# First attention with the first half's routing and the shared expert: one hand-kept order of steps per engine, in place of a fixed step pattern with insertions

## The chip, the cores and the metric

One NeuronCore of a Trainium2 chip runs the whole kernel. The metric is the device time of one execution in microseconds (us). A core has five engines with their own instruction streams: TensorE (PE; its weight loads are listed as PEld), VectorE (DVE), ScalarE (ACT), GpSimd (POOL) and SyncE (SP, which issues most DMAs). Each engine takes its instructions in the order in which the program lists them and waits at semaphores for the others.

## The reference, cut to what matters

A two-layer decoder on 16 sequences of 128 tokens with 128 features. The change lies between the second and the third line:

```
x = x + L0_attn(layernorm(x))                        # gated recurrence with its feed-forward
x = x + L0_xattn(layernorm(x), ctx, ctx, mask)       # attention: 16 heads of 8, rotary
x = x + L0_ffn(layernorm(x))                         # shared expert + 8 experts, top 2
x = x + L1_attn(layernorm(x))
x = x + L1_xattn(ctx, ctx, layernorm(x), mask)
x = x + L1_ffn(layernorm(x))
```

with, inside `L0_xattn` and `L0_ffn`,

```
scores = einsum('bhqd,bhkd->bhqk', qh, kh) / sqrt(8)
out = einsum('bhqk,bhkd->bhqd', softmax(masked scores), vh)
concat @ Wo + bo
...
shared = (silu(x @ shared_gate.T) * (x @ shared_up.T)) @ shared_down.T
probs = sigmoid(x @ router_w.T + routing_bias);  scores, indices = top_k(probs, 2)
combined = sum over the two experts of score * ((silu(x @ gate_e) * (x @ up_e)) @ down_e)
```

## The kernel before, in words

**Attention (`attention(0)`, a = 0).** It runs over 8 steps n, each of two sequences with all 16 heads. The queries and keys of a step, split into three bf16 parts, lie in DRAM (`q_scr`, `k_scr`) and are loaded into one of three slots. Each engine has its own list of small pieces of work, named here by kind, number and step, as in A3.2 (kind A, number 3, step 2):

- PE: A0 to A7 are groups of scores of four heads each (`scores`, L2070), each with one matmul of the identity ahead of it (`keep_warm`, L1854); M turns the row maxima (`m_rows`, L2114); B0 to B3 are the transposed scores, which contain the maxima by way of rows written into the query slot (`scores_T`, L2088); V0 to V3 are exponentials times values (`values_sum`, L2104); X0, X1 transpose the products (`products_T`, L1746); o0, o1 transpose the normalised heads (`out_rows`, L2129).
- DVE: x0 to x7 reduce the groups A0 to A7 to maxima (L1363); P splits the maxima in two bf16 parts (L1369, L1370); E copies the turned maxima (L1374), after which SP writes them into the query slot (L462) and issues the loads of the step after the next (L434, L436); N0, N1 normalise (L1384, L1386).
- ACT: e0 to e3 are the exponentials of B0 to B3 (L955); K0, K1 copy the products out (L965); s0, s1 store the output (L970).
- POOL: c0, c1 lay out the values (L637).

A1.n and the later groups take turns in two PSUM banks, B in two pairs of banks, V writes bank U, and M, X and o take turns in the single bank T: a piece that writes T waits until the reader of the piece before it in T is done.

**The order of the pieces.** A table `STEP[0]` gives the order of the pieces within a step, the same for all engines; an engine does those of the pieces that are its own. A piece of step n stands together with some of step n + 1 (the A, P, M and E of n + 1) and n - 1.

**Mixture steps.** Output projection, residual, layer norm, router and shared expert of `L0_xattn` and `L0_ffn` are done in four blocks of four sequences. Their steps are named by kind and block. In the order of their dependence: po (PE, output projection, 2 passes, L1782), oc (ACT, L1016), bk (PE, turned back, L1778), ad (DVE, added to x, L1457), sa and sb (DVE, statistics, L1461 to L1467), rs (POOL, 1/sqrt, L657, L658), nr (DVE, normalise, L1472), tr (PE, transpose, L1778), nt (ACT, L1019), ro (PE, router, L2016), lg (DVE, L1477). From nt the shared expert goes on: sg and su (PE, gate and up, L2036), sl (ACT, silu, L1028), hd (DVE, product, L1547), so (PE, down, L2044), sd (DVE, added to x, L1550). From lg of two blocks the routing of half of the tokens goes on: pr (ACT, L1022), ta and tb (DVE, the best two experts, L1485 to L1496), cu (PE, counts, L2022, L2023), cc (DVE, L1499), ps (DVE, places of the rows, L1502 to L1524), te (DVE, the expert of each tile, L1529 to L1533), wt (DVE, weights, L1535 to L1537). gc (DVE) copies the weights of the first three tiles' experts (`gu_copy`, L1434, L1437).

A mixture step of an early block is put behind a named piece of the attention by the table `BESIDE` ("4A6": "tr.0" puts tr.0 behind the place of A6 in step 4's pattern); what is left stands in the three parts of the list `CLOSE` behind and between the last pieces. `ORDER`, which the waits between mixture steps are counted from, is made of both tables.

**What follows.** POOL scatters the normalised rows of the first eight sequences to their places in DRAM (16 indirect DMAs, L711, after ps.0; rs.3 stands between the first eight and the last eight), SP loads them back (L470), and a loop over 46 tiles of routed rows begins on PE (L2220 gate and up, L2232 down), ACT (L1058) and DVE (L1437 copies an expert's weights, L1571 the product). Tile x needs the product of tile x - 2 (L1571); tiles 0 and 1 need sd.2 and sd.3.

## Time and profile before

| | |
|---|---|
| median of 3 runs | 776.41 us (775.45 to 781.89) |
| the profiled execution | 780.67 us, of which the span of its instructions 778.9 us |
| PE busy over the span | 77% |
| VectorE, ScalarE, GpSimd busy | 56%, 38%, 30% |
| mean granted TensorE clock | 0.878 of full speed |
| first attention, first piece to last value sum | 127.8 to 243.8 us |
| from there to the third routed tile on PE | 243.8 to 291.0 us |

Times are microseconds from the first instruction of the profiled execution. Of TensorE's clock, 1.00 is 2.4 GHz and 0.50 is 1.2 GHz; a value between them is a mix of the two over a stretch. PE's matmuls are pipelined, and the profile models their ends, so a piece's price on PE is read as the distance from its start to the start of the next piece while PE does not wait.

### The profile page before, as it was taken

What the parts mean: (1) busy time and instruction counts of PE and PEld (TensorE: products, weight loads), DVE (VectorE), ACT (ScalarE), POOL (GpSimd) and SP (SyncE); (2) the same over time, 40 slices, a digit from 0 to 9 for tenths busy, and PEclk for the clock granted to TensorE, in tenths of its full rate; (3) what the DMA queues carried; (4) which work ended last, traced back from release to release, by engine and by line L of the source; (5) the groups of instructions that cost most, each with busy time, mean ns of one, the idle gap of its engine ahead of it and who ended that gap; (6) DMA issues with size and microseconds to landing.
All of it is one profiled execution on the core that took longest, in us unless ns stands there. A gap on an engine that the chain in (4) does not pass through costs nothing.

```text
span 778.9 us, 15307 instructions
## 1 busy us (share of the span) xinstructions
PE 601.5 (77%) x4751; PEld 432.5 (56%) x4751; DVE 438.5 (56%) x1165; ACT 296.2 (38%) x679; POOL 232.9 (30%) x324
## 2 busy tenths in 40 slices
PE   4699996898778849898716699846799987555992
PEld 2444453665555639798504488623466764534992
DVE  4889787566554554356334566355455642568443
ACT  2585320455334314343202277511145453101661
POOL 6735333001004545243621111022100001353452
PEclk9899998899996989999866899976799997657997
DMA  9955987543200083432100000108543500003014
GB/s 286 323 93 155 274 216 221 130 115 84 66 4 21 30 313 96 122 107 67 47 24 1 0 2 1 50 14 239 131 114 84 127 2 1 0 32 105 25 35 129
DMA packets 87492, 75.71 MB, mean 97 GB/s; under 512 B 10456, under 2 KB 80752, under 8 KB 84512
## 3 DMA queue, kind: packets, MB, share of 16 engines
q1 hardware_dynamic: 82544, 66.80, 31.7%
q0 software_dynamic: 3296, 6.79, 2.9%
q10 hardware_dynamic: 1584, 1.26, 0.5%
q8 instruction: 37, 0.61, 0.3%
q14 instruction: 31, 0.25, 0.1%
HBM read 41.59 MB, written 32.98 MB: 96 GB/s over the span
## 4 chain that ended last, share of the span: by engine, by line
PE 44%; DVE 20%; issue 11%; DMA 7%; POOL 6%; ACT 3%; SPq 3%; another core or an unknown queue 2%; DVEq 2%; POOLq 0%; ACTq 0%
PE ps L2220 5%; PE ps L2104 4%; PE ps L1782 3%; PE ps L1746 3%; PE ps L2088 2%; PE ps L2070 2%; SPq L426 2%; POOL xs_scr L779 2%; PE ps L2323 2%; PE ps L2232 2%; DMA q_scr<-parts 2%; PE ps L1930 2%; PE ps L2066 2%; PE ps L2083 2%
## 5 line engine op out<-in xcount | busy, mean ns | idle before, releaser
L1363 DVE TENSOR_REDUCE negm<-ps 128x4 f32<-128x512 f32 x128 | 85.1, 689 | 63.0 <-PE ps L2070 60.6
L955 ACT ACTIVATE wa<-ps 128x1024 f32<-128x1024 f32 x64 | 65.6, 1025 | 83.0 <-PE ps L2088 80.8
L2220 PE MATMUL ps<-nT,f 128*128 128x128 f32 x368 | 52.3, 287 | 11.3 <-DVE wb L1571 8.4
L2220 PEld LDWEIGHTS ps<-nT,f 128*128 128x128 f32 x368 | 47.1, 200 | 13.7 <-DVE wb L1571 10.0
L2104 PE MATMUL ps<-wa,f 128*32 128x128 f32 x1024 | 42.9, 294 | 2.9 <-ACT wa L955 1.9
L1854 PE MATMUL ps<-identb 128*128 128x512 bf16 x108 | 38.6, 418 | 4.8 <-issue 2.1
L2070 PE MATMUL ps<-stack 75*128 75x128 bf16 x384 | 40.6, 232 | 0.0
L2070 PEld LDWEIGHTS ps<-stack 75*128 75x128 bf16 x384 | 32.4, 105 | 14.6 <-issue 4.8
L711 POOL DMA_INDIRECT x_scr<-y_tok,selT x32 | 31.5, 985 | 28.0 <-ACT stack L1064 18.8
L2088 PE MATMUL ps<-stack 75*128 75x128 bf16 x384 | 35.5, 231 | 2.2 <-DMA stack<-mT 1.5
L784 POOL DMA_INDIRECT y_scr<-f,stack x23 | 25.8, 1121 | 31.5 <-DVE f L1721 21.1
L1058 ACT ACTIVATE wa<-ps 128x256 f32<-128x256 f32 x46 | 17.8, 388 | 44.8 <-PE ps L2220 42.1
L2088 PEld LDWEIGHTS ps<-stack 75*128 75x128 bf16 x384 | 28.9, 104 | 10.2 <-issue 2.8
L2104 PEld LDWEIGHTS ps<-wa,f 128*32 128x32 f32 x1024 | 26.1, 115 | 12.6 <-issue 5.5
L1100 ACT ACTIVATE wa<-ps,rec 128x128 f32<-128x128 f32 x92 | 26.3, 371 | 17.3 <-PE ps L2323 17.3
L1437 DVE COPY f<-w_gu 128x512 f32 x46 | 20.8, 452 | 20.0 <-issue 14.0
L1746 PE MATMUL ps<-ident,xn_tm 128*128 128x128 f32 x32 | 8.9, 432 | 29.8 <-DVE xn_tm L1129 26.3
L1571 DVE TENSOR_TENSOR wb<-wa,ps 128x256 f32<-128x256 f32 x46 | 19.2, 417 | 22.1 <-ACT wa L1058 19.3
L965 ACT ACTIVATE f<-ps 128x512 f32<-128x512 f32 x32 | 19.1, 598 | 32.0 <-PE ps L2104 31.8
L637 POOL COPY f<-v2x 128x144 f32 x16 | 4.9, 307 | 85.1 <-ACTq L963 84.5
L2232 PE MATMUL ps<-w_down,wb 128*128 x184 | 29.7, 286 | 0.7 <-ACT stack L1064 0.5
L637 POOL COPY f<-v0x 128x144 f32<-128x144 f32 x16 | 4.8, 306 | 82.9 <-ACTq L963 82.6
(391 smaller groups left out, 1508.8 us busy)
## 6 DMA issues: line engine op xcount, KB each, us to landing
k_scr<-parts SPq DMA_DIRECT2D x48, 192.0 KB, 3.0
q_scr<-parts SPq DMA_DIRECT2D x48, 192.0 KB, 3.5
stack<-k_scr SPq DMA_DIRECT2D x12, 600.0 KB, 7.0
stack<-q_scr SPq DMA_DIRECT2D x12, 600.0 KB, 5.3
w_w<-in_w SPq DMA_DIRECT2D x2, 2048.0 KB
x_scr<-sel SPq DMA_DIRECT2D x2, 1472.0 KB, 10.3
x_scr<-stack SPq DMA_DIRECT2D x10, 256.0 KB, 4.9
wb<-q_scr SPq DMA_DIRECT2D x4, 600.0 KB, 5.0
```

Of the source, the lines that this page charges most:

```text
L711: g.indirect_dma_start(x0_scr[h], bass.IndirectOffsetOnAxis(ap=pos0_i[:, k * B + b:k * B + b + 1], axis=0), y_tok[:, b, :], None).then_inc ...
L784: g.indirect_dma_start(y_scr, bass.IndirectOffsetOnAxis(ap=xs[:, x, D:D + 1].bitcast(i32), axis=0), ys[:, x, :], None).then_inc(ys_scatter ...
L955: link.release(act.activation(wa[:, u % 2, :], BF[u % 2], ACT.Exp, scale=SCALE), hWA.filled, hWA.at(stage, n * 4 + u), hB.freed)
L1100: last = act.activation(gelu_of[x % NW1][:, c * S:(c + 1) * S], A[x % 2][:, c * S:(c + 1) * S], ACT.Gelu, bias=b1_of[x % NW1][:, c:c + 1])
L1363: v.tensor_reduce(negm[:, g4 * 4:g4 * 4 + 4, j], A[u % 2].rearrange("p (h k) -> p h k", h=4), AX.X, ALU.max, negate=True).then_inc(hA.free ...
L1746: last = tr(T[:, j * S:(j + 1) * S], src(j), ident[:, :])
L1854: mm(bank, identb[:, :], identb[:, :].unsqueeze(1).broadcast_to([128, 4, S]), start=True, stop=True)
L2070: last = mm(bank[:, q * S:(q + 1) * S], qst[s][0:NROW, h, j * S:(j + 1) * S], kst[s][0:NROW, h, j * S:(j + 1) * S], start=(a == 0), stop=T ...
L2088: last = mm(bank[:, q * S:(q + 1) * S], kst[s][0:NROW, h, j * S:(j + 1) * S], qst[s][0:NROW, h, j * S:(j + 1) * S], start=(a == 0), stop=True,
L2104: last = mm(U[rows, cols], v_batch[j][:, h * VC:h * VC + 32], wa[:, u % 2, q * S:(q + 1) * S], start=True, stop=True)
L2220: last = mm(A[x % 2][:, c * S:(c + 1) * S], gu_of[x % NGU][:, c * S:(c + 1) * S], nT[:, k % 2, q * S:(q + 1) * S], start=True, stop=True)
L2232: last = mm(Bk[y % 2][:, 1, 0:D], hid_of[y % NGU][:, c * S:(c + 1) * S], w["down"][:, 1:, c, :][:, bass.ds(chosen, 1), :].rearrange("p o d ...
```

## The change

Both tables go. In their place stands `WOVEN`, with for each engine one list of all pieces of the first attention and all mixture steps, piece by piece. The lists hold the same pieces as before on each engine (198 on PE, 136 on DVE, 78 on ACT); no instruction of the attention or of a mixture step is added or taken out, and the identity matmul ahead of each group of scores stands in both kernels. The second attention keeps its pattern. Beside the order, four things differ:

- po.2, bk.2, tr.2 and ro.2 use the second score bank (A[1]); before, po.2 and bk.2 used T, tr.2 and ro.2 used U.
- The 16 scatters of the first half are two named steps of POOL's list, fa.0 and fb.0; one short GpSimd instruction that stood ahead of them now stands behind.
- x0 of a step waits also until the last maxima were turned into parts, which is the same engine's own earlier work.
- so.1, which writes A[1], waits also for lg.2, which reads it.

```diff
+        def of_attention(step):
+            return step[1].isdigit()
-        ORDER = {eng: FRONT[eng] + [s for n in range(NSTEP) for op, u in STEP[0] for s in extra(eng, n, op, u)]
-                 + [s for part in CLOSE[eng] for s in part.split()] for eng in FRONT}
+        ORDER = {eng: FRONT[eng] + [s for s in WOVEN[eng] if not of_attention(s) and s[:2] not in ("fa", "fb")]
+                 for eng in FRONT}
...
+        T_TURN = {s: k for k, s in enumerate(s for s in WOVEN["PE"] if s[0] in "MXo" and of_attention(s))}
...
-            return U if step in ("tr.2", "ro.2", "bk.3", "ro.3", "cu.1") else T
+            return dict(T=T, U=U, Z=A[1])[bank_name(step)]
+        def bank_name(step):
+            return "Z" if step in ("po.2", "bk.2", "tr.2", "ro.2") else "U" if step in ("bk.3", "ro.3", "cu.1") else "T"
...
+                    for s in WOVEN["POOL"]:
+                        if of_attention(s):
+                            copies(int(s[3]), int(s[1]))
+                        elif s in ("fa.0", "fb.0"):
+                            first_rows("ab".index(s[1]))
+                        else:
+                            mixture_step(s[:-2], int(s[-1]))
...
+            def first_rows(part):
+                g.wait_ge(zero0_stored, 32)
+                g.wait_ge(dve_front, after("ps.0"))
+                for b in range(part * HB // 2, (part + 1) * HB // 2):
+                    scatter(b, 0)
...
+                    if a == 0 and u == 0 and n > 0:
+                        v.wait_ge(mp_ready, n)
...
+                    if n == 1:
+                        pe.wait_ge(dve_front, after("lg.2"))
...
+                if a == 0:
+                    for s in WOVEN["PE"]:
+                        kind, n = s[:-2], int(s[-1])
+                        if not of_attention(s):
+                            mixture_step(kind, n)
+                            continue
+                        u = int(kind[1])
+                        if kind[0] == "A":
+                            scores(n, u, n % 3, n // 3)
+                        elif kind[0] == "B":
+                            scores_T(n, u, n % 3)
...
-BESIDE = {
-    "PE": {"3A6": "po.0", "3B2": "bk.0", "4A6": "tr.0", "4A7": "ro.0", "4B2": "po.1", "5A0": "bk.1", "5B2": "tr.1",
...
+WOVEN = {
+    "PE": """
+            A0.0 A1.0 A2.0 A3.0 A4.0 A5.0 A6.0 A7.0 A0.1 A1.1 M0.0 A2.1 A3.1 A4.1 A5.1 A6.1 B0.0 A7.1 B1.0
...
```

What this does to the instructions is shown at three places. A line number is one of the file it stands in; the same work has other numbers in the two files (scores L2070 and L2077, transposed scores L2088 and L2095, value sums L2104 and L2111, identity L1854 and L1862).

The first place is PE in the middle, where tr.0, ro.0 and po.1 are done. Before, from A6 of step 5 on (L1778 is tr.0, L2016 ro.0, L1782 po.1):

```order
L1854 MATMUL ps<-identb 128x512
L2070 MATMUL ps<-f,wb 128x128 x4
L1778 MATMUL ps<-ident,y_tok 128x128 x4
L2104 MATMUL ps<-wa,f 32x128 x8
L1854 MATMUL ps<-identb 128x512
L2070 MATMUL ps<-f,wb 128x128 x4
L2016 MATMUL ps<-w_router,nT 128x8 x4
L2088 MATMUL ps<-stack 128x128 x8
L1782 MATMUL ps<-y_tok,w_wo 128x512
L2088 MATMUL ps<-stack 128x128 x8
```

Now, from A6 of step 5 on (L1790 is po.1, L1786 tr.0):

```order
L1862 MATMUL ps<-identb 128x512
L2077 MATMUL ps<-f,wb 128x128 x4
L1790 MATMUL ps<-y_tok,w_wo 128x512
L1862 MATMUL ps<-identb 128x512
L2077 MATMUL ps<-f,wb 128x128 x4
L2095 MATMUL ps<-stack 128x128 x16
L1786 MATMUL ps<-ident,y_tok 128x128 x4
```

po.1 moved ahead of tr.0, and ro.0 moved out of the step, behind five groups of scores of the next.

The second place is PE at the end of the attention. Before, from X0.7 on (L2036 x4 is sg.0 with su.0, the second L1746 X1.7, L1778 tr.2, L1782 po.3, L2016 ro.2, L2044 so.0):

```order
L1746 MATMUL ps<-ident,f 128x128 x4
L2104 MATMUL ps<-wa,f 32x128 x8
L2129 MATMUL ps<-ident,o_tok 128x128
L2104 MATMUL ps<-wa,f 32x128 x8
L2036 MATMUL ps<-nT,w_gu 128x512 x4
L1746 MATMUL ps<-ident,f 128x128 x4
L1778 MATMUL ps<-ident,y_tok 128x128 x4
L2129 MATMUL ps<-ident,o_tok 128x128
L1782 MATMUL ps<-y_tok,w_wo 128x512
L2036 MATMUL ps<-nT,w_gu 128x512 x2
L2016 MATMUL ps<-w_router,f 128x8 x4
L2044 MATMUL ps<-w_down,wb 128x128 x8
```

Now, from sg.0 on (L2027 and L2028 are cu.0, the second L2041 su.0, the second L1754 X1.7):

```order
L2041 MATMUL ps<-nT,w_gu 128x512 x2
L1754 MATMUL ps<-ident,f 128x128 x4
L2111 MATMUL ps<-wa,f 32x128 x16
L2027 MATMUL ps<-pick,earlier 128x64
L2028 MATMUL ps<-pick,ones 128x64
L2041 MATMUL ps<-nT,w_gu 128x512 x2
L2136 MATMUL ps<-ident,o_tok 128x128
L1786 MATMUL ps<-ident,y_tok 128x128 x4
L2041 MATMUL ps<-nT,w_gu 128x512 x2
L1754 MATMUL ps<-ident,f 128x128 x4
L2021 MATMUL ps<-w_router,f 128x8 x4
L2136 MATMUL ps<-ident,o_tok 128x128
```

sg.0 moved ahead of the last value sums, and cu.0, which stood between B2.6 and B3.6, behind them.

The third place is DVE at the end of the mixture steps. Before, from the last copy of gc.0 on (L1550 is sd.2, L1547 hd.3, L1499 cc.1, the second L1550 sd.3, L1502 the start of ps.1):

```order
L1437 COPY f<-w_gu 128x512
L1550 TENSOR_TENSOR x_tok<-x_tok,ps 128x512
L1547 TENSOR_TENSOR wb<-wa,ps 128x1024
L1499 COPY xn_tm<-ps 128x128
L1550 TENSOR_TENSOR x_tok<-x_tok,ps 128x512
L1502 SCALAR_TENSOR_TENSOR xn_tm<-ones,xn_tm 128x64
```

Now, from the end of tb.1 (L1505) on (L1556 is hd.3, L1508 cc.1, L1511 the start of ps.1):

```order
L1505 TENSOR_TENSOR pick<-pick 128x8x8
L1556 TENSOR_TENSOR wb<-wa,ps 128x1024
L1508 COPY xn_tm<-ps 128x128
L1511 SCALAR_TENSOR_TENSOR xn_tm<-ones,xn_tm 128x64
L1512 TENSOR_TENSOR xn_tm<-xn_tm 128x64
```

and, further on, at the end of te.1 (L1542; L1559 is sd.3, what follows wt.0):

```order
L1540 TENSOR_REDUCE selT<-xn_tm 128x23
L1541 TENSOR_SCALAR selT<-selT 128x23
L1542 CAST selT<-selT 128x23
L1559 TENSOR_TENSOR x_tok<-x_tok,ps 128x512
L1544 TENSOR_TENSOR wsum<-top_p 128x16
L1545 RECIPROCAL wsum<-wsum 128x16
```

sd.3 moved from ahead of ps.1 to behind te.1; gc.0 moved up to between hd.0 and lg.2, sd.2 to ahead of ta.1, and ps.0 with te.0 from ahead of sa.2 to behind nr.2.

## Rows read from the trace of the kernel before

**Rows 1.** Busy time by stretch: stretch, its us, each engine, granted clock, DMA share

```profile
147.70:158.30 10.60, 9.70 (x148) 7.07 (x148) 7.15 (x16) 6.16 (x9) 0.61 (x2) 1.00 0.51 120
158.30:168.60 10.30, 9.66 (x147) 7.09 (x148) 6.72 (x14) 5.52 (x9) 0.61 (x2) 1.00 0.51 123
168.60:181.50 12.90, 11.39 (x154) 7.81 (x153) 7.62 (x16) 6.90 (x10) 0.61 (x2) 1.00 0.39 98
181.50:196.00 14.50, 12.70 (x163) 8.81 (x162) 9.49 (x29) 7.03 (x10) 1.84 (x4) 1.00 0.37 88
196.00:212.60 16.60, 12.48 (x156) 8.74 (x155) 10.07 (x29) 6.45 (x9) 1.81 (x4) 0.91 0.32 77
212.60:229.60 17.00, 14.13 (x161) 10.05 (x161) 10.61 (x31) 6.80 (x10) 0.61 (x2) 0.89 0.01 2
229.60:243.80 14.20, 11.35 (x129) 7.95 (x129) 8.37 (x38) 6.13 (x9) 1.84 (x4) 0.64 0.01 2
```

**Rows 2.** Timeline of PE at full clock: start, us, operation, idle before

```profile
161.44 0.38 PE L1854 MATMUL ps<-identb 128*128 128x512 bf16 x1
...
161.88 0.61 PE L2088 MATMUL ps<-wb,f 75*128 75x128 bf16 x8
162.32 0.38 PE L1854 MATMUL ps<-identb 128*128 128x512 bf16 x1
...
163.75 0.64 PE L2104 MATMUL ps<-wa,f 128*32 128x128 f32 x16
164.33 0.33 PE L2129 MATMUL ps<-ident,o_tok 128*128 128x128 f32 x1
...
184.21 0.63 PE L1746 MATMUL ps<-ident,f 128*128 128x128 f32 x4 [0.38 <-ACTq L95]
...
222.98 1.10 PE L1782 MATMUL ps<-y_tok,w_wo 128*128 128x512 f32 x2 [0.28 <-ACTq L95]
```

**Rows 3.** Groups of instructions, 127 to 284 us: count, busy, mean ns, idle before

```profile
L1363 DVE TENSOR_REDUCE negm<-ps 128x4 f32<-128x512 f32 x64 | 42.9, 689 | 27.1 <-PE ps L2070 25.1
L955 ACT ACTIVATE wa<-ps 128x1024 f32<-128x1024 f32 x32 | 32.8, 1025 | 37.9 <-PE ps L2088 35.9 <-ACT wa L955 2.0
```

**Rows 4.** Timeline of VectorE's closing part, idle time before each; then PE's load

```profile
234.27 0.29 DVE L1502 TENSOR_TENSOR_SCAN xn_tm<-ones,xn_tm 128x64 f32<-128x64 f32 x1
...
239.33 0.49 DVE L1461 BATCH_NORM_STATS2 bn<-x_tok 128x6 f32<-128x128 f32 x2 [0.24 <-DVE selT L1533]
...
243.15 1.11 DVE L1472 TENSOR_SCALAR y_tok<-x_tok,mv,rstd 128x128 f32<-128x128 f32 x4 [0.94 <-POOLq L659]
...
249.76 0.26 DVE L1384 RECIPROCAL rec<-ps 128x16 f32<-128x16 f32 x1 [5.50 <-issue]
...
255.03 0.19 DVE L1477 TENSOR_TENSOR rl<-ps,rbias 128x32 f32<-128x32 f32 x1 [3.25 <-PE ps L2036]
...
257.36 0.69 DVE L1457 TENSOR_TENSOR x_tok<-x_tok,ps 128x512 f32<-128x512 f32 x1 [2.13 <-PE ps L1778]
...
281.94 0.69 DVE L1550 TENSOR_TENSOR x_tok<-x_tok,ps 128x512 f32<-128x512 f32 x1 [3.09 <-PE ps L2044]
...
290.53 0.41 DVE L1571 TENSOR_TENSOR wb<-wa,ps 128x256 f32<-128x256 f32 x1
291.00 1.78 PEld L2220 LDWEIGHTS ps<-nT,f 128*128 128x128 f32 x8 [5.61 <-DVE wb L1571]
```

**Rows 5.** Timeline of GpSimd's scatters and SyncE's load; its landing time, median us

```profile
244.57 1.24 POOL L711 DMA_INDIRECT x_scr<-y_tok,selT  x1 [0.98 <-DVEq L1551]
...
262.87 1.03 POOL L711 DMA_INDIRECT x_scr<-y_tok,selT  x1 [0.88 <-POOL rstd L658]
...
274.24 1.43 SPq L470 DMA_DIRECT2D stack<-x_scr  x2
...
stack<-x_scr SPq DMA_DIRECT2D x2, 256.0 KB, 2.8
```

**Rows 6.** The chain that ended last: one load of a step's keys

```profile
149.88 8.29 DMA stack<-k_scr
```

192 lines of the change are left out of this document (102 added, 90 removed), and 16 rows, old and new, of tables (BESIDE, CLOSE, STEP).

## The prediction

> **What bounds the kernel now.** I read the busy time by stretch first, cut at the starts of the steps on PE [rows 1]. In the two steps that hold no mixture step (147.7 to 168.6) a step takes 10.6 and 10.3 us, and PE is busy 9.70 and 9.66 of them: 93%. These steps are bound by PE, with VectorE at 7 us. The steps with mixture steps take 12.9, 14.5, 16.6 and 17.0 us, and the last value sums another 14.2: from 168.6 to 243.8 there are 75.2 us, in which PE is busy 11.39 + 12.70 + 12.48 + 14.13 + 11.35 = 62.05 (83%), VectorE 46.2. No engine is full there: they wait for each other in turn. In the group table VectorE sat idle 27.1 us before them and ScalarE 37.9 us before its exponentials [rows 3]. The granted clock says a second thing: 1.00 up to 196.0, then 0.91, 0.89 and 0.64, so part of the later stretches ran at 1.2 GHz. The timeline of the closing part says a third: VectorE carries the chain to the routed loop, and sits idle in it for 5.50, 3.25, 2.13 and 3.09 us; the loop's third tile starts at 291.00, after a PE wait of 5.61 us for the first product on VectorE (290.53) [rows 4].
>
> So the change acts on three pieces: the steps up to 168.6, the middle (75.2 us) and the closing part (243.8 to 291.0, 47.2 us). Everything behind 291.0 follows in the same order and shifts with it.
>
> **Prices on PE.** From starts at full clock: a group of scores with its identity 161.44 to 161.88, 0.44; a B 161.88 to 162.32, 0.44; a V 163.75 to 164.33, 0.58. An X is four transposes, at most the 0.63 of its row, I take 0.5; po is 1.1 [rows 2]. The o and M are single transposes, 0.15 (estimate, a quarter of X). A plain step is 8 A, 4 B, 4 V, 2 X, 2 o and M: 3.5 + 1.8 + 2.3 + 1.0 + 0.5 = 9.1 us, against the 10.3 measured, a factor of 1.14.
>
> **The change, part by part.**
>
> *The start.* B0.0 waits for SyncE's write of the turned maxima, in both orders. Now three more groups of scores stand ahead of it (A4.1 to A6.1), work that was to be done anyway, while B0.0 itself gets at most one group later. M comes one to three V and X earlier in steps 1 and 2, which starts SyncE's load earlier. Gain: 0 to 3 us. I take 0.5, since PE was already busy 93% in the steps that follow.
>
> *The middle.* No work is added, so I cost what may be recovered. Were all waits as short as in the plain steps, the 62.05 us of busy PE would take 62.05/0.93 = 66.7 us: 8.5 less. The part at 1.2 GHz, twice (1 minus granted): 2 x (0.09 x 16.6 + 0.11 x 17.0 + 0.36 x 14.2) = 17.0 us, in which PE did the work of 8.5. With PE denser this could go too, so the most to be had is 17 us. The least is nothing. To choose between them I count the new lists by stretch:
> - A0.4 to A0.5: 8 A, 5 V, 5 B, po's successor bk.0, 2 X: PE 10.6, VectorE 7.0 (a plain step [rows 1]) plus ad, sa and sb of a block.
> - A0.5 to A0.6: PE 8.7, with two B and two V fewer held back; VectorE 8. The same stretch took 14.5 us before.
> - A0.6 to A0.7: VectorE is the longest. Block work of sa, sb, nr, lg and then ad, sa, sb, nr lies in the two stretches 181.5 to 212.6, whose busy time exceeds two plain steps by 9.49 + 10.07 - 13.9 = 5.7 us, so a block is 3.2 busy, about 4.4 with the pauses between its chained pieces. 7.0 + 0.7 of pauses + 0.7 for a third N + 4.4 = 12.8 us (16.6 before).
> - A0.7 to A7.7: PE 5.6, VectorE 6.6.
> - From there to V3.7: ScalarE is the longest, with eight exponentials of 1.03 [rows 3] and 0.2 of handoff each (estimate from the plain steps), and about 6 us of copies and of pr.0 between them: 16 us.
>
> The longest engine's sum from A0.4 on is 11.2 + 8.7 + 12.8 + 6.6 + 16 = 55.3. Before, measured over the longest engine's count was 12.9/10.4, 14.5/11.6 and 16.6/12.1: 1.24 to 1.37, the last one at a lowered clock. The order was made with handoffs in view (V stands farther behind its B, an X behind other work), and I take 1.15, the factor of the plain steps: 63.6 us instead of 75.2, a gain of 11.6. At 1.25 it is 69.1, a gain of 6; at 1.0, 20.
>
> The bank T is a limit of its own: po, bk, tr and ro hold it from PE's write to the reader's end, about 1.1 + 0.7 + two handoffs of 0.2 for po. The move of po.2 and bk.2 to A[1] takes some 3.7 us of such holds out of it. It costs nothing: A[1] has no group of scores left by then, and A7.7's maximum was read before.
>
> A rule of the Trainium skill is weighed here. "TensorE: Matmul & The Clock Gate", section on HAM oscillation, puts the loss by a lowered clock at the throttled time times one half, 17.0/2 = 8.5 us in this stretch. The rows bear it out only in part: 181.5 to 196.0 ran at 1.00 throughout and still took 1.25 times its longest engine. By the rule alone the middle would gain 8.5; my sum doesn't use it.
>
> *The loads.* SyncE writes M's rows for step n, then issues the loads of step n + 2, whose keys land 8.29 us later [rows 6]; with the issue of both about 10.5 us from E.n to A0.(n + 2). M0.3 is now behind A1.4 and B3.2. From it to A0.5 PE has 6 A, 5 V, 4 B, 2 X, bk.0 and small ones, 9.5 us, so A0.5 may wait 1 us; M0.5 to B0.5 and M0.6 to B0.6 (3.7 and 2.7 us of PE against about 3.7 for turn, copy and SyncE's write) up to 1 us each. Behind a waiting A0.5 stands all of PE. Up to 3 us, inside the factor of 1.15.
>
> *The closing part.* Let V be the end of V3.7 (243.8 before). Before, VectorE went from ps.0 at 234.27 to the end of product 0 at 290.94, 56.7 us [rows 4]. Of it, sa.2, sb.2, N0.7 and nr.2 (239.33 to 244.26, 4.9) now stand ahead of ps.0. N1.7, for which it idled 5.50, now stands behind nr.2, cc.0, ps.0 and te.0, over 6 us of work, so that wait is covered. lg.2 (3.25) has hd.0 and gc.0 ahead of it, ad.3 (2.13) hd.1. sd.3 (3.09), which waited for so.3, stands behind ps.1 and te.1. If that cover failed, each would come back at its own size. All four gone: 14.0. I add 2 for new waits, at hd.2 and hd.3, because sg.3, su.3 and so.2 now come one behind the other on PE. 56.7 - 4.9 - 14.0 + 2 = 39.8. But cu.0 now stands behind V3.7, so ps.0 starts about 2 after V, where before it started 9.5 ahead. The loop's third tile then stands at V + 42, 47.2 before: a gain of 5.4. What follows next is the rows' way: POOL's 16 scatters took 10.1 (244.57 to 254.7) and 9.9, and waited for rs.3 between; without a wait SyncE issues at about ps.0's end + 23.5, and with 2.8 for landing [rows 5] the rows are there at V + 6 + 26.5 = V + 32.5, 9 us ahead of need. Bounds: 0 (all four waits return elsewhere) and 9.
>
> **The sum.** 0.5 + 11.6 + 5.4 = 17.5, rounded to 18. The profiled execution, 780.7, would become 762.7; it lies 4.3 above the median, so 776.4 - 18 = **758.5 us**.
>
> **The rivals.**
> - *The waits only move (B).* An in-order list with waits sized for other durations stalls elsewhere, and the middle gains 0 to 2; the closing waits are separate and go. For it: the steps with mixture work have no full engine, yet were not dense. Against: the stretches after A0.5 lose work outright. 776.4 - 7 = 769.
> - *The closing gain is lost (C).* ps.0 is later against V, and the scatter chain of 26.5 us or rs.3 between gets on the path. It decides once ps.0 ends later than V + 15. Middle alone: 776.4 - 12 = 764.5.
> - *All of it (D).* Factor 1.0 to 1.05 in the middle: -17 to -20, and -8 in the closing: 750.
> - *No effect (E).* Both only shuffle: 776.
> - *Slower, by the clock (F).* From A7.7 on no identity matmuls are left, and more B, V and sg work stands there, 13.6 + about 27 of PE at full clock up to so.3. If the short waits between these keep PE at 1.2 GHz, each us of it costs another. Before, 17.0 of the 48 us ahead of 243.8 were at 1.2 GHz. To end slower the lowered clock must cover over 26 us more than before, for it has to outweigh 18; throughout from A0.6, 55 us of work would take 110, and the kernel about 795. Against it: rows 1 show 1.00 wherever PE was busy over 86%. A rule speaks for it: the same page of the Trainium skill, section "A second HAM failure mode: psum-queue depth-cycling", says that short pauses between groups that cycle PSUM banks make the clock alternate. The plain steps here cycle banks too, and stay at 1.00.
>
> **How the numbers follow.** Forecast (752 to 765): 0.55. B 0.17, C 0.10, D 0.10, E 0.04, F 0.04. Under 1% (7.8 us, about what a measurement of this kernel tells from no change) nothing counts as faster: forecast, C, D and a good third of B are over it, 0.82; the rest of B and E within it, 0.14; F 0.04. For 8 in 10 I leave out E, F, half of D and the slow third of B: 750 to 769.
>
> **What would show it.** In the profile after: steps 2 and 3 at 10 us as before; A0.5 to A0.7 in about 25 us, not 31.1; V3.7's end near 232; granted clock over 0.9 up to there; VectorE's wait before so.3's reader gone and none over 2 us behind ps.0; the third tile near 273. Wrong if the middle keeps 83% of busy PE, if the loads show as PE's releaser for over 3 us, or if ps.0 ends later than V + 8.

## The result and the profile after

The changed kernel takes 759.17 us (median of four runs, 754.92 to 764.65), beside 779.15 us for the kernel before on the same chip (775.45 to 785.72). The ratio is 0.971, with a 95% interval of 0.966 to 0.976: 20 us less, where 18 were forecast (758.5). The profiled execution of the changed kernel took 754.92 us, with a span of 753.2. The ratios in this document leave out executions more than 1.5% above the fastest of the same kernel, which concerns three of the ten of before_no_identity (788.7 to 790.0 us) and no others.

Busy time by stretch, after, cut at the starts of the steps on PE as in [rows 1] (stretch, its us, PE, PE's loads, VectorE, ScalarE, GpSimd, granted clock, DMA share, GB/s). The first row starts with A0.2, the third with A0.4, the last two hold A7.7 to the end of V3.7, and the closing part:

```profile
146.70:157.10 10.40, 9.59 (x147) 6.93 (x147) 6.53 (x15) 5.25 (x7) 0.31 (x1) 1.00 0.38 86
157.10:166.60 9.50, 9.20 (x128) 6.56 (x125) 6.00 (x12) 5.51 (x8) 0.61 (x2) 1.00 0.56 132
166.60:179.95 13.35, 11.66 (x178) 8.56 (x176) 9.62 (x30) 6.87 (x9) 1.84 (x4) 1.00 0.40 97
179.95:189.45 9.50, 9.14 (x120) 6.56 (x117) 7.39 (x17) 5.17 (x8) 0.61 (x2) 1.00 0.53 132
189.45:202.90 13.45, 12.69 (x197) 9.72 (x195) 10.18 (x30) 7.69 (x11) 1.81 (x4) 1.00 0.40 94
202.90:210.30 7.40, 6.12 (x64) 4.25 (x63) 5.08 (x11) 2.00 (x3) 0.31 (x1) 1.00 0.03 6
210.30:228.90 18.60, 14.72 (x219) 10.35 (x217) 9.58 (x37) 11.22 (x17) 1.82 (x4) 1.00 0.01 3
228.90:271.80 42.90, 33.00 (x160) 22.30 (x160) 29.60 (x94) 12.98 (x18) 25.72 (x35) 0.92 0.32 111
```

V3.7 ends at 228.9 (243.8 before), the clock is at its upper level throughout up to there, and the third routed tile starts 42.9 us later (47.1 before). So the kernel is 15 us ahead at the first mark and 19.2 at the second. Everything behind runs the same code; the profiled execution is 25.7 us shorter in the end, but the last 6.5 of it lie behind, in code that didn't change, and the medians differ by 20.0.

The groups of instructions that answer to [rows 3], 127 to 265 us (count, busy, mean ns, idle before): the maxima still number 64, and VectorE sits idle 19.2 us ahead of them instead of 27.1, while ScalarE's idle time ahead of its exponentials is as it was.

```profile
L1372 DVE TENSOR_REDUCE negm<-ps 128x4 f32<-128x512 f32 x64 | 42.0, 687 | 19.2 <-PE ps L2077 16.5 <-DVE bn L1470 0.2
L966 ACT ACTIVATE wa<-ps 128x1024 f32<-128x1024 f32 x32 | 32.7, 1023 | 37.7 <-PE ps L2095 33.5 <-ACT wa L966 1.2 <-PE ps L2111 1.0
```

The timeline of VectorE in the closing part, after (start, us, operation, idle before and its releaser), which answers to [rows 4]:

```profile
228.00 0.26 DVE L1393 RECIPROCAL rec<-ps 128x16 f32<-128x16 f32 x1 [2.93 <-PE ps L1754]
...
230.43 0.29 DVE L1511 TENSOR_TENSOR_SCAN xn_tm<-ones,xn_tm 128x64 f32<-128x64 f32 x1
...
235.57 0.26 DVE L1393 RECIPROCAL rec<-ps 128x16 f32<-128x16 f32 x1 [0.26 <-DVE selT L1542]
...
240.63 0.18 DVE L1486 TENSOR_TENSOR rl<-ps,rbias 128x32 f32<-128x32 f32 x1
...
252.05 0.19 DVE L1486 TENSOR_TENSOR rl<-ps,rbias 128x32 f32<-128x32 f32 x1 [1.21 <-PE ps L2021]
254.44 0.69 DVE L1559 TENSOR_TENSOR x_tok<-x_tok,ps 128x512 f32<-128x512 f32 x1 [2.20 <-PE ps L2051]
...
268.65 0.69 DVE L1559 TENSOR_TENSOR x_tok<-x_tok,ps 128x512 f32<-128x512 f32 x1
```

These are N0.7, ps.0, N1.7, lg.2, lg.3, sd.2 and sd.3. ps.0 stands 1.5 us behind V3.7. N1.7's wait fell from 5.50 to 0.26, and those of lg.2 (3.25) and sd.3 (3.09) are gone; ad.3 has none either. New are 2.20 at sd.2, 1.21 at lg.3 and 2.93 at N0.7.

### The profile page after: what moved, and what is told of

Read it like the earlier page. It is cut to its first block, busy times and chain, and to the rows that moved or that the text cites. A ratio compares the mean times of both kernels' runs of the same rounds, so it can differ in the third digit from the quotient of the medians.

```text
span 753.2 us, 15317 instructions
## 1 busy us (share of the span) xinstructions
PE 588.2 (78%) x4751; PEld 421.9 (56%) x4751; DVE 438.9 (58%) x1165; ACT 294.9 (39%) x679; POOL 232.4 (31%) x324
## 3 DMA queue, kind: packets, MB, share of 16 engines
q0 software_dynamic: 3296, 6.79, 2.9%
## 4 chain that ended last, share of the span: by engine, by line
PE 48%; DVE 19%; issue 11%; DMA 6%; ACT 4%; POOL 4%; SPq 3%; another core or an unknown queue 2%; DVEq 2%; POOLq 0%; ACTq 0%
PE ps L2234 4%; PE ps L2111 4%; PE ps L1790 3%; PE ps L1754 3%; PE ps L2077 3%; PE ps L2095 2%; SPq L432 2%; PE ps L2246 2%; DMA q_scr<-parts 2%; ACT wa L966 2%; PE ps L1938 2%; PE ps L2073 2%; PE ps L2337 2%; PE ps L2090 2%
## 5 line engine op out<-in xcount | busy, mean ns | idle before, releaser
L2234 PE MATMUL ps<-nT,f 128*128 128x128 f32 x368 | 50.6, 281 | 8.9 <-DVE wb L1579 4.8
L2234 PEld LDWEIGHTS ps<-nT,f 128*128 128x128 f32 x368 | 45.6, 195 | 11.2 <-DVE wb L1579 6.1
L1862 PE MATMUL ps<-identb 128*128 128x512 bf16 x108 | 41.0, 436 | 13.3 <-issue 8.1
L2111 PE MATMUL ps<-wa,f 128*32 128x128 f32 x1024 | 39.1, 278 | 4.9 <-ACTq L95 2.2
L2077 PE MATMUL ps<-stack 75*128 75x128 bf16 x384 | 39.1, 226 | 0.0
L2077 PEld LDWEIGHTS ps<-stack 75*128 75x128 bf16 x384 | 31.3, 101 | 13.7 <-issue 3.1
L2095 PE MATMUL ps<-stack 75*128 75x128 bf16 x384 | 33.3, 223 | 0.6 <-DMA stack<-mT 0.6
L1065 ACT ACTIVATE wa<-ps 128x256 f32<-128x256 f32 x46 | 17.7, 385 | 39.8 <-PE ps L2234 39.5
L1107 ACT ACTIVATE wa<-ps,rec 128x128 f32<-128x128 f32 x92 | 26.1, 369 | 16.9 <-PE ps L2337 16.9
L2111 PEld LDWEIGHTS ps<-wa,f 128*32 128x32 f32 x1024 | 24.9, 110 | 12.9 <-ACT wa L966 5.3
L1754 PE MATMUL ps<-ident,xn_tm 128*128 128x128 f32 x32 | 8.8, 431 | 29.9 <-DVE xn_tm L1136 26.3
L2095 PEld LDWEIGHTS ps<-stack 75*128 75x128 bf16 x384 | 26.9, 100 | 8.3 <-issue 2.1
L1579 DVE TENSOR_TENSOR wb<-wa,ps 128x256 f32<-128x256 f32 x46 | 19.2, 418 | 20.3 <-ACT wa L1065 16.1
L1862 PEld LDWEIGHTS ps<-identb 128*128 128x128 bf16 x108 | 11.3, 106 | 30.3 <-issue 21.1
## 6 DMA issues: line engine op xcount, KB each, us to landing
x_scr<-sel SPq DMA_DIRECT2D x2, 1472.0 KB, 10.3
```

The costliest lines, as they stand in the source:

```text
L1107: last = act.activation(gelu_of[x % NW1][:, c * S:(c + 1) * S], A[x % 2][:, c * S:(c + 1) * S], ACT.Gelu, bias=b1_of[x % NW1][:, c:c + 1])
L1754: last = tr(T[:, j * S:(j + 1) * S], src(j), ident[:, :])
L1862: mm(bank, identb[:, :], identb[:, :].unsqueeze(1).broadcast_to([128, 4, S]), start=True, stop=True)
L2077: last = mm(bank[:, q * S:(q + 1) * S], qst[s][0:NROW, h, j * S:(j + 1) * S], kst[s][0:NROW, h, j * S:(j + 1) * S], start=(a == 0), stop=T ...
L2095: last = mm(bank[:, q * S:(q + 1) * S], kst[s][0:NROW, h, j * S:(j + 1) * S], qst[s][0:NROW, h, j * S:(j + 1) * S], start=(a == 0), stop=True,
L2111: last = mm(U[rows, cols], v_batch[j][:, h * VC:h * VC + 32], wa[:, u % 2, q * S:(q + 1) * S], start=True, stop=True)
```

## The experiments

Four marks in the trace of each kernel tell where its time went: E.3, E.6 and E.7 (VectorE's copy of the turned maxima of steps 3, 6 and 7), V (the end of V3.7) and T (the third routed tile on PE). The first column is the time against the kernel before on the same chip. The marks come from one profiled execution each, and V and T are good to about 0.1 us.

| kernel | ratio (95%) | E.3-E.6 | E.6-E.7 | E.7-V | V-T |
|---|---|---|---|---|---|
| before | 1 | 44.0 | 17.2 | 14.0 | 47.1 |
| changed | 0.971 (0.966 to 0.976) | 36.3 | 8.8 | 15.5 | 42.9 |
| tail_old | 0.985 (0.978 to 0.992) | 36.3 | 8.5 | 16.8 | 52.2 |
| mid_old | 0.987 (0.978 to 0.996) | 46.0 | 18.5 | 12.4 | 41.4 |
| splice_e6 | 0.984 (0.979 to 0.990) | 45.1 | 9.7 | 15.4 | 42.5 |
| mix_old | 0.992 (0.990 to 0.995) | 44.5 | 16.5 | 16.6 | 43.4 |
| att_old | 0.995 (0.992 to 0.997) | 44.1 | 18.9 | 16.9 | 42.9 |
| e7_late | 0.979 (0.973 to 0.985) | 36.3 | 12.6 | 18.1 | 41.7 |
| banks_old | 0.978 (0.972 to 0.985) | 36.3 | 8.5 | 19.4 | 42.4 |
| no_identity | 0.973 (0.966 to 0.980) | 35.0 | 11.2 | 16.5 | 42.5 |
| before_no_identity | 0.998 (0.994 to 1.002) | 45.2 | 18.7 | 13.4 | 47.2 |
| before_warm | 0.998 (0.994 to 1.001) | 45.2 | 20.7 | 13.4 | 48.0 |
| sg0_behind_x | 0.970 (0.967 to 0.973) | 36.3 | 8.6 | 15.0 | 41.7 |
| two_moves | 0.973 (0.968 to 0.978) | 36.3 | 8.5 | 16.3 | 42.6 |

E.3 lies between 167.4 and 170.4 in all of them (before 168.70, changed 168.33). One per cent of the ratio is 7.8 us.

### The closing part alone, and the rest alone

tail_old keeps the changed kernel up to N1.7 and puts the order of before behind it. On two of the engines (ScalarE's list is put back in the same way):

```diff
 VectorE, behind N1.7
-hd.0 gc.0 lg.2 hd.1 ad.3 sa.3 sb.3 sd.0 sd.1 nr.3 hd.2 lg.3 sd.2 ta.1 tb.1 hd.3 cc.1 ps.1 te.1 sd.3 wt.0
+hd.0 lg.2 ad.3 sa.3 sb.3 sd.0 hd.1 nr.3 sd.1 hd.2 lg.3 ta.1 tb.1 gc.0 sd.2 hd.3 cc.1 sd.3 ps.1 te.1 wt.0
 PE, behind o0.7
-tr.2 sg.1 X1.7 ro.2 o1.7 po.3 su.1 bk.3 so.0 so.1 sg.2 su.2 tr.3 ro.3 so.2 sg.3 su.3 cu.1 so.3
+X1.7 tr.2 o1.7 po.3 sg.1 ro.2 so.0 bk.3 su.1 sg.2 so.1 tr.3 su.2 ro.3 sg.3 so.2 su.3 cu.1 so.3
```

> The changed kernel with the order of before put back behind o0.7 on PE, N1.7 on VectorE and K1.7 on ScalarE (the closing part alone), the new order up to there. Theory (two separate gains, 15 in the middle and 4.2 in the closing part): the waits of VectorE at lg.2, ad.3 and sd.3 come back (3.25, 2.13 and 3.09 before, less what short new waits of the new tail go), V3.7 still ends near 229, the third tile stands at V + 47, and the kernel takes 4 to 6 us more than the changed one, 764. Rival (the closing gain came only from what was moved ahead of V3.7, not from the order behind it): the third tile at V + 43, within 1.5 us of the changed kernel, 759.

It takes 0.985 of before, some 10 us more than the changed kernel where 4 to 6 were expected, and nearly all of it lies where the order was put back: V stands at 229.6, T 52.2 us behind. VectorE's waits there, in the timeline of tail_old:

```profile
243.28 0.19 DVE L1486 TENSOR_TENSOR rl<-ps,rbias 128x32 f32<-128x32 f32 x1 [4.90 <-PE ps L2041]
246.58 0.69 DVE L1466 TENSOR_TENSOR x_tok<-x_tok,ps 128x512 f32<-128x512 f32 x1 [3.11 <-PE ps L1786]
...
273.07 0.69 DVE L1559 TENSOR_TENSOR x_tok<-x_tok,ps 128x512 f32<-128x512 f32 x1 [3.49 <-PE ps L2051]
```

lg.2, ad.3 and sd.3 wait 4.90, 3.11 and 3.49 us: the same three waits as in [rows 4], each a little larger. The theory had V + 47; it missed that ps.0, which stood 9.5 us ahead of V before, is behind it now (231.21, V + 1.6). From ps.0 to the end of product 0 VectorE takes 50.6 us here; before, it took 56.7, of which 4.9 were pieces that now stand ahead. So the old tail costs 5 us more behind V than it did in its own kernel.

mid_old is the counterpart: the order of before up to V3.7, N1.6 and K1.7, the new one behind.

```diff
 VectorE
-... P0.7 lg.1 E0.7 N0.6 ta.0 tb.0 N1.6 ad.2 sa.2 sb.2 N0.7 nr.2 cc.0 ps.0 te.0 N1.7 hd.0 ...
+... tb.0 x7.7 P0.7 cc.0 N0.6 E0.7 ad.2 N1.6 sa.2 sb.2 N0.7 nr.2 ps.0 te.0 N1.7 hd.0 ...
```

> The counterpart: the order of before up to V3.7 on PE, N1.6 on VectorE and K1.7 on ScalarE, the new order behind it; tr.2 and ro.2 use A[1], po.2 and bk.2 stay on T. Theory: V3.7 ends near 243.8 as before, the closing part gains 3 to 5 us, so 773 to 775 where before is 777 to 779. Rival (closing and middle gains depend on each other, since cu.0, sg.0 and bk.2 have moved between the two): no gain or a loss, 777 or more, with N1.7 or ps.0 waiting for what now stands late on PE.

0.987 of before. V stands at 245.3, 1.5 later than before, and T 41.4 behind it (47.1 before): T is 4.2 us earlier. That is the net gain of the closing part on its own, in the trace, and bears the theory out; the ratio, with its wide interval, would allow 3 to 17. By the ratios the two parts (1.5% and 1.3%) add up to the whole (2.9%); by the traces, 9.1 and 4.2 us at T, 6 of the 19.2 us need both. The intervals don't decide between these.

splice_e6 has the order of before up to M0.6, E0.6, e3.5 and rs.1, and the new one behind.

```diff
 PE
-... X0.5 A0.7 A1.7 M0.6 A2.7 X1.5 A3.7 A4.7 tr.1 A5.7 B0.6 ...
+... tr.1 B3.5 X0.5 V2.5 M0.6 V3.5 A0.7 A1.7 A2.7 X1.5 A3.7 A4.7 A5.7 B0.6 ...
```

> The order of before up to M0.6 on PE, E0.6 on VectorE, e3.5 on ScalarE and rs.1 on POOL, the changed kernel's order behind it. Theory (the gain is made stretch by stretch, and most of it behind E.6): E.6 near 212.7 as before, V3.7 24.3 us after it (31.2 before), third tile 43 after V3.7, so 11 us less than before and 8 to 9 more than the changed kernel, 768. Rival (the new order needs its own state ahead of it, since steps held back before are late behind the cut): E.6 to V3.7 28 us or more, 772 to 777.

768.92 us, 0.984. E.6 stands at 213.2, and V 25.1 us behind it (31.1 before, 24.3 in the changed kernel). So the gain behind E.6 doesn't need the new order ahead of it. Of the middle's gain, 7.7 us are made from E.3 to E.6 and 6.9 behind.

### Is it the clock?

Before, the last three stretches of the middle ran at 0.91, 0.89 and 0.64 [rows 1], and the changed kernel runs them at 1.00. Does the order gain because it keeps the clock up? before_warm tries to buy the clock alone:

```diff
                     pe.wait_ge(hB.freed, hB.at(stage, n * 4 + u))
+                    if a == 0 and n > 4:
+                        keep_warm(Bk[u % 2][:, 0, :], n // 7 + 1)
```

> The kernel before, in its own order, with one more identity matmul of 4 x 128 columns ahead of each of the four B groups of steps 5 and 6, and two ahead of each in step 7: 16 matmuls of 0.22 us, 3.5 us of added PE work; the output is unchanged. Theory (order): the lowered clock from 196 to 243.8 was a consequence of the waits; the waits are between engines and stay, so the added work buys the clock at most in part, and the time is 0 to 3 us longer. Rival (clock): the 17.0 us at 1.2 GHz, in which PE did the work of 8.5, were what the middle lost; with the granted clock at 1.00 the kernel gains 8.5 - 3.5 = 5 us or more though no step is moved.

The time is that of before (0.998, 0.994 to 1.001), and in the profiled execution the clock wasn't bought. Busy time by stretch of before_warm, E.5 to E.6 and E.6 to E.7:

```profile
196.30:213.60 17.30, 14.40 (x160) 9.89 (x159) 10.17 (x29) 6.44 (x9) 1.82 (x4) 0.84 0.29 74
213.60:234.30 20.70, 19.42 (x169) 13.46 (x173) 10.81 (x31) 6.79 (x10) 0.62 (x2) 0.64 0.01 2
```

So this trace says nothing on what a clock at 1.00 would give. It is also the least favourable of the ten executions: its mean clock is 0.868, their median 0.884, and 0.873 is the median of the kernel before's thirteen beside them. In the others some clock may have been bought, then, though no time beyond the interval. mid_old says more on the price of a lower clock, by chance: up to V3.7 it has the order of before, and its clock was lower than before's. The same two stretches of mid_old:

```profile
196.60:214.50 17.90, 14.25 (x156) 10.10 (x155) 10.09 (x30) 6.38 (x9) 1.81 (x4) 0.81 0.29 71
214.50:232.90 18.40, 16.87 (x165) 11.61 (x168) 10.70 (x31) 6.79 (x10) 0.61 (x2) 0.72 0.01 3
```

At 1.2 GHz ran 2 x (0.19 x 17.9 + 0.28 x 18.4) = 17.1 us of them, in the profile of before 2 x (0.09 x 16.6 + 0.11 x 17.2) = 6.8. The two stretches took 36.3 and 33.8 us. So 10.3 us more at the lower clock came with 2.5 us more of time, a quarter, if all of the difference is put down to the clock: PE was busy 31.12 us instead of 26.79, and shorter waits took up much of the difference. A second pair gives less. E.7 to V has the same order in before and in before_no_identity (below), and no group of scores in it: 14.0 us at 0.63 (10.4 us at 1.2 GHz) and 13.4 us at 1.00, so there the lower clock came with 0.6 us. The Trainium skill ("TensorE: Matmul & The Clock Gate", section on HAM oscillation) counts half of the throttled time as lost; that is more than these traces show, where PE is not full. By these two pairs, an estimate, the 17.0 us at 1.2 GHz were worth 2 to 4 of the middle's 15 us.

no_identity takes the identity matmuls away from the changed kernel:

```diff
-                    if a == 0 and True:
+                    if a == 0 and False:
                         keep_warm(bank, 1)
```

> The changed kernel without the identity matmul ahead of each group of scores of the first attention: 64 matmuls of 0.22 us, 14 us of PE work less; the output is unchanged. If the order alone makes the gain, PE is shorter by up to 12 us in the steps bound by it and the kernel is faster, 750 to 759. If the clock is what the identity matmuls buy, the granted clock in the steps falls to 0.5 to 0.8, each us at 1.2 GHz costs up to half, and the kernel takes 10 to 40 us more, 770 to 800.

0.973, where the changed kernel has 0.971: the same within the intervals, and neither of the two expected ranges (750 to 759, 770 to 800) holds its median of 761.0. The granted clock was lower in these two stretches of no_identity (E.6 to E.7, E.7 to V), where the changed kernel has 1.00:

```profile
204.40:215.50 11.10, 10.69 (x99) 9.23 (x100) 5.74 (x14) 3.90 (x5) 0.00 (x0) 0.58 0.02 3
215.50:232.00 16.50, 13.46 (x162) 8.74 (x162) 7.67 (x32) 8.73 (x14) 1.82 (x4) 0.87 0.01 2
```

They hold 2 x (0.42 x 11.1 + 0.13 x 16.5) = 13.6 us at 1.2 GHz, nearly the 17.0 of before, and E.3 to V still takes 62.7 us (75.2 before, 60.6 changed). So 12.5 of the 14.6 us that the order gains there are gained with nearly as much time at 1.2 GHz as before. These 12.5 contain what the missing identity matmuls save; the next kernel takes that out.

before_no_identity is the same edit on the kernel before.

> The kernel before without the identity matmul ahead of each group of scores of the first attention (14 us of PE work less; the output is unchanged). Without it the changed kernel stood at 0.973 of before. If order and identity are independent, this kernel lies within 0.5% of before, 778 to 784, and the order's gain without identity is again 18 us or so. Rival (the old order, with more waits on PE, needs the identity matmuls to keep the clock, and the new one does not): 790 or more.

0.998 (0.994 to 1.002): no measurable difference. E.3 to V takes 77.3 us, against 62.7 in no_identity: without identity matmuls the order gains 14.6 us there, as it does with them. So the gain doesn't hang on them, and at the prices above most of it isn't the clock's either. That leaving them out changes nothing doesn't mean that they do nothing. From E.3 to E.7 before_no_identity has 32 of them fewer and runs 2 x (0.11 x 15.1 + 0.35 x 17.0 + 0.42 x 18.7) = 30.9 us at 1.2 GHz instead of 6.8, and takes 63.8 us instead of 61.2; from E.1 to E.3 it takes 20.0 instead of 20.9. Less work and less clock may cancel.

### The attention's order, or the places of the mixture's steps?

mix_old keeps the attention's pieces in the new order and puts the mixture steps back where they stood. Some of the edits on VectorE:

```diff
 VectorE
-E0.6 x1.7 x2.7 N1.5 x3.7 x4.7 x5.7 x6.7 x7.7 P0.7 lg.1 E0.7 N0.6 ta.0 tb.0 N1.6 ad.2 ... cc.0 ps.0
+E0.6 x1.7 lg.1 x2.7 N1.5 x3.7 x4.7 ta.0 x5.7 x6.7 tb.0 x7.7 P0.7 cc.0 E0.7 N0.6 ad.2 N1.6 ps.0
```

> The changed kernel with the attention's own steps in the new order, but each step of the mixture up to V3.7 put back behind the attention step that it followed before (po.1, tr.1, ro.1, po.2, bk.2, oc.0, oc.2, nt.1 and ad.2 one to four places later, where the bank T's turns leave no other; po.2 and bk.2 on T again). Theory P (places of the mixture's steps make the middle gain, because each of them makes PE wait for a reader when it stands too near its producer): V3.7 ends near 240, and the kernel takes 7 to 11 us more than the changed one, 766 to 770. Rival A (the attention's own order makes it, V farther behind its B): V3.7 within 3 us of 229, 759 to 762.

att_old has the attention as before and the mixture steps behind the neighbours of the changed kernel.

```diff
 PE
-A1.6 V2.4 M0.5 A2.6 V3.4 X0.4 A3.6 A4.6 ro.0 A5.6 B0.5 bk.1 B1.5
+X0.4 V2.4 M0.5 A0.6 V3.4 A1.6 o0.4 A2.6 X1.4 A3.6 B0.5 A4.6 ro.0 bk.1 B1.5
```

> The counterpart: the attention's steps in the order of before, the mixture's steps up to V3.7 behind the attention step that they follow in the changed kernel (ad.0, bk.1, nt.1 and sg.0 moved by one or two places for the turns of the banks); closing part new. Theory P: most of the middle gain is here, V3.7 ends near 232, 760 to 763. Rival A: V3.7 ends at 240 or later, 768 to 772.

Both expectations fell. Neither half makes any of the middle's gain: E.3 to E.6 takes 44.5 and 44.1 us, before 44.0, the changed kernel 36.3; V stands at 245.8 and 250.0. Both kernels also have po.2 and bk.2 back on T and some steps moved by a place or more for the banks' turns, so they aren't pure halves; banks_old below shows no cost of T ahead of E.7. The new tail alone (mid_old) gave at least as much as either. What halves do to each other can be read in mix_old, where ta.0 stands among the maxima, but pr.0, its input, comes from a ScalarE that itself waits for PE. Timeline of VectorE in mix_old:

```profile
217.30 0.69 DVE L1372 TENSOR_REDUCE negm<-ps 128x4 f32<-128x512 f32 x1 [0.16 <-PE ps L2077]
220.52 0.20 DVE L1494 TENSOR_SCALAR pr<-pr 128x64 f32<-128x64 f32 x1 [2.52 <-ACT pr L1029]
...
223.00 1.29 DVE L1372 TENSOR_REDUCE negm<-ps 128x4 f32<-128x512 f32 x2
```

PE's next group of scores waits for these maxima, and ScalarE in its turn waits 6.79 us for PE. The timelines of PE and ScalarE:

```profile
223.75 0.61 PE L1862 MATMUL ps<-identb 128*128 128x512 bf16 x1 [4.17 <-DVE negm L1372]
...
228.19 1.02 ACT L966 ACTIVATE wa<-ps 128x1024 f32<-128x1024 f32 x1 [6.79 <-PE ps L2111]
```

One late input among the maxima held all three engines in turn. That accounts for part of E.6 to E.7 (16.5 us instead of 8.8); which waits make the 8.2 us more from E.3 to E.6 isn't shown here. In the changed kernel ta.0 stands behind E0.7, with nothing of the attention behind it but three normalisations.

e7_late tests that place by itself. Only M0.7 and its reader are moved, behind the neighbours that they had before:

```diff
 PE
-V0.6 V1.6 M0.7 B3.6 o1.5 V2.6 X0.6 po.2
+V0.6 V1.6 B3.6 o1.5 V2.6 X0.6 M0.7 po.2
 VectorE
-P0.7 lg.1 E0.7 N0.6 ta.0
+P0.7 lg.1 N0.6 E0.7 ta.0
```

> The changed kernel with one link of the last score chain put back by a few places: M0.7 on PE behind X0.6 instead of ahead of B3.6, and its reader E0.7 on VectorE behind N0.6 instead of ahead of it, as the two stood to each other before. Theory C (E.n sets the pace: its write to memory releases all of B.n and so ScalarE's exponentials, and the gain of E.6 to E.7, 17.2 to 8.8 us, comes from E0.7 having neither N0.6 nor the mixture's pieces ahead of it): E.7 3 to 4 us later, V3.7 as much, 762 to 763. Rival (the exponentials have slack there): V3.7 within 1 us of E.n as before, 759.

0.979, 6 us more than the changed kernel by the ratios, whose intervals overlap; 5.1 us from E.3 to T in the traces. E.6 is unmoved, E.7 comes 3.8 us later (12.6 instead of 8.8), and V another 2.6 (18.1 instead of 15.5). VectorE's timeline in e7_late: P0.7, lg.1, then N0.6 waits 3.93 us for X0.6, with E0.7 behind it.

```profile
210.78 0.19 DVE L1379 TENSOR_TENSOR mp<-negm,mp 128x32 bf16<-128x32 f32 x1
210.98 0.19 DVE L1486 TENSOR_TENSOR rl<-ps,rbias 128x32 f32<-128x32 f32 x1
215.11 0.26 DVE L1393 RECIPROCAL rec<-ps 128x16 f32<-128x16 f32 x1 [3.93 <-PE ps L1754]
...
216.27 0.22 DVE L1383 COPY mT<-ps 64x128 bf16<-64x128 bf16 x1 [0.41 <-PE ps L2121]
```

In the changed kernel P0.7's last piece stands at 212.03 and E.7 at 213.41, 1.4 us later; here it is 5.5. E.n releases the write to memory, and with it all of B.n and the exponentials, and in this trace what stands between P and E came out at V in full and more. The theory holds, and its size (3 to 4) was short by 2.6 at V: the granted clock in the stretch behind was 0.72 instead of 1.00 as well.

### The bank

banks_old takes po.2 and bk.2 back to T, tr.2 and ro.2 to U. In the changed order bk.2 can't use T as it stands: X1.6 behind it would wait for ad.2, which on VectorE stands behind X1.6's own reader. So X1.6 goes first:

```diff
-return "Z" if step in ("po.2", "bk.2", "tr.2", "ro.2") else "U" if step in ("bk.3", "ro.3", "cu.1") else "T"
+return "U" if step in ("tr.2", "ro.2", "bk.3", "ro.3", "cu.1") else "T"
 PE
-B0.7 B1.7 bk.2 X1.6 V0.7
+B0.7 B1.7 X1.6 bk.2 V0.7
```

> The changed kernel with po.2 and bk.2 back on the bank T and tr.2 and ro.2 on U as before; X1.6 stands ahead of bk.2, since behind it X1.6 would wait for a reader that stands behind X1.6's own. Theory (the move to A[1] costs nothing and takes 3.7 us of holds out of T): 1 to 4 us more than the changed kernel, 760 to 763. Rival (the holds lie beside the exponentials, which set that stretch): within 1 us, 759.

0.978, 5 us more than the changed kernel (the intervals overlap). The trace places it: E.7 to V takes 19.4 us instead of 15.5, everything ahead is equal. The 3.9 us are about the size of the holds that the prediction named (3.7). They are the price of T together with the new place of X1.6, at a granted clock of 0.91 instead of 1.00; no run separates these.

### Two tries for more

sg0_behind_x exchanges two neighbours, since in the changed kernel's timeline of PE sg.0 waits for the last exponential with X0.7 behind it:

```profile
225.43 1.98 PE L2041 MATMUL ps<-nT,w_gu 128*128 128x512 f32 x4 [2.49 <-ACTq L95]
```

```diff
 PE
-o1.6 sg.0 X0.7 V2.7 V3.7 cu.0
+o1.6 X0.7 sg.0 V2.7 V3.7 cu.0
```

> The changed kernel with two neighbours on PE exchanged: X0.7 ahead of sg.0. In the changed kernel's trace sg.0 waits 2.49 us for the last exponential (it writes the banks that e3.7 reads), with X0.7 behind it, for which VectorE then waits 2.93 at N0.7. If that wait is on the path, N0.7, nr.2, cc.0 and ps.0 come 2 us earlier and the kernel takes 1 to 2.5 us less, 757. Rival: ps.0 waits for cu.0, which stands behind V3.7 in any case, and V3.7 for e3.7, so only N0.7 moves and the time stays within 0.7 us, 759.

E.7 to T is 1.7 us shorter in the trace (56.75 instead of 58.43), the ratio is 0.970 beside 0.971. A gain of that size is below what the intervals tell apart; it isn't shown. two_moves adds a second one:

```diff
 VectorE
-hd.2 lg.3 sd.2 ta.1 tb.1 hd.3 cc.1
+hd.2 lg.3 ta.1 tb.1 sd.2 hd.3 cc.1
```

> The changed kernel with X0.7 ahead of sg.0 on PE (1.7 us less from E.7 to the third tile in the trace where it was moved alone) and sd.2 behind tb.1 on VectorE, where it waited 2.20 us for so.2. If both waits are on the path to the third tile: 3 to 4 us less than the changed kernel, 755 to 756. Rival (hd.3 waits for su.3 in any case, so the second wait only moves to hd.3): 1 to 2 us less, 757 to 758.

No gain (0.973), and both expectations fell. ps.1 did come earlier, at 261.21 and not 262.09, but T is at 272.55: E.7 to T takes 58.9 us, with 58.4 in the changed kernel and 56.75 in sg0_behind_x. The chain that ended last in two_moves, up to the second routed tile's products on PE (start, us, engine or transfer), shows what stands there now:

```profile
258.37 2.77 DMA x_scr<-y_tok,selT
261.20 0.40 SPq L476
261.81 8.08 DMA stack<-x_scr
269.94 1.11 PE ps L2216 x4
```

Ahead of these rows it holds the sixteen scatters, back to the first at 235.48. L2216 turns the routed rows in groups of four tiles, the second group right behind tile 0 and ahead of tile 1, in order. PE waits there for the rows that GpSimd scatters and SyncE loads, 2.57 us for the first group and 2.47 for the second. The timeline of PE in two_moves:

```profile
264.22 0.63 PE L2216 MATMUL ps<-ident,stack 128*128 128x128 f32 x4 [2.57 <-DMA stack<-x_scr]
...
269.94 1.11 PE L2216 MATMUL ps<-ident,stack 128*128 128x128 f32 x4 [2.47 <-DMA stack<-x_scr]
270.84 2.82 PE L2234 MATMUL ps<-nT,f 128*128 128x128 f32 x16
```

The last row holds the second and the third tile, eight matmuls each and one right behind the other; the ninth starts at 272.55. Product 0, for which the third waits, was done at 270.97 already. So here the rows set T.

In the changed kernel the chain up to T is still VectorE's (up to its product 0):

```profile
268.65 0.70 DVE x_tok L1559
...
271.40 0.40 DVE wb L1579
271.84 1.16 PE ps L2234 x8
```

But the scatters have little slack there either. The timelines of GpSimd, SyncE and PE in the changed kernel, which answer to [rows 5]:

```profile
234.89 1.24 POOL L665 DMA_INDIRECT x_scr<-y_tok,selT  x1 [8.20 <-DVEq L1560]
...
248.76 1.03 POOL L665 DMA_INDIRECT x_scr<-y_tok,selT  x1 [0.95 <-DVEq L1560]
...
257.71 0.96 POOL L665 DMA_INDIRECT x_scr<-y_tok,selT  x1 [0.30 <-issue]
...
260.00 1.39 SPq L476 DMA_DIRECT2D stack<-x_scr  x2
...
268.48 0.66 PE L2216 MATMUL ps<-ident,stack 128*128 128x128 f32 x4 [0.84 <-DMA stack<-x_scr]
```

From ps.0 at 230.43 this chain takes 4.5 us to the first scatter, 23.8 to the end of the sixteenth, 1.3 to SyncE's issue and 8.5 to the turn of the second group: 38.1 us, and T comes 3.4 behind, after PE waited 1.18 us for product 0. In two_moves it is 38.9 and 2.6, in mid_old 38.2 and 3.1 (ps.0 at 245.49, the second group's turn at 283.64). So with ps.0 where it is, T can gain little more than a microsecond from VectorE's order; no run shortened the scatters or the loads, or turned the second group later (its rows are first used by tile 4), and what that would give is open.

## Why the prediction was right, and where it was not

- *What bounds the kernel.* "These steps are bound by PE" (the plain steps, at 93% busy) was too strong. before_no_identity takes 16 identity matmuls of 0.22 us (3.5 us) out of them (E.1 to E.3) and gains 0.9 there, 20.0 us (PE 17.03 busy, clock 0.95) instead of 20.9 (19.37, 1.00). In the mixture steps of the new order it is alike: no_identity takes 24 (5.3 us) out of E.3 to E.6 and gains 1.3.
- *The start.* Forecast 0.5, measured 0.4 at E.3. The new order led by 5.7 us at E.1 (142.10, before 147.77) and had lost nearly all of it by E.3; that VectorE's work was early bought nothing lasting there.
- *The middle.* The step that carried the sum: the longest engine's work times 1.15, stretch by stretch.

| stretch | longest engine's sum | forecast (x 1.15) | measured |
|---|---|---|---|
| A0.4 to A0.5 | 11.2 | 12.9 | 13.35 |
| A0.5 to A0.6 | 8.7 | 10.0 | 9.50 |
| A0.6 to A0.7 | 12.8 | 14.7 | 13.45 |
| A0.7 to A7.7 | 6.6 | 7.6 | 7.40 |
| A7.7 to V3.7 | 16 | 18.4 | 18.60 |
| sum | 55.3 | 63.6 | 62.3 |

The factor came out at 1.13. PE is busy 54.3 of the 62.3 us, 87%, where it was 83%, and A0.5 to A0.7 take 22.95 us ("about 25" forecast, 31.1 before). V3.7's end was forecast near 232 and stands at 228.9; 2 of the 3 us are there because A0.4 stands 2 us earlier in the new order than before (166.6 and 168.6). Rival B, that the waits only move, fell with the table, though mix_old and att_old show it to be real: with only one half of the order put in, the middle gained nothing.

  Part of the closeness is luck. The count named VectorE as the longest engine from A0.6 to A7.7 (12.8 and 6.6 us) and ScalarE behind (16). By busy time in the profile after, PE is the longest in all five stretches: 12.69, 6.12 and 14.72 us in these three, where VectorE has 10.18 and 5.08 and ScalarE 11.22. The counts of the other two contain pauses that were estimated, so the sum of 55.3 lies near PE's 54.3 without having come from it. And the first term, 11.2, has no working of its own: the list beside it gives PE 10.6, with which the sum would be 54.7 and the forecast for the middle 62.9.
- *The bank* was costed at nothing, with 3.7 us of holds saved; banks_old, which moves X1.6 as well, takes 3.9 more.
- *The loads.* Three waits of up to 1 us were allowed (A0.5, B0.5, B0.6). One of them came, 0.56 us at B0.6, and one not named, 0.65 at A0.2. Right in size.
- *The clock* was forecast over 0.9 up to V3.7 and was 1.00. Rival F (slower by the clock) had named A7.7 to so.3 as the place: 1.00 up to V3.7 and 0.92 behind. Half of the throttled time, 17.0/2 = 8.5 us for the old losses, was too much; the runs give 2 to 4. Nor does "1.00 wherever PE was busy over 86%" hold beyond [rows 1]: in no_identity PE was busy 10.69 of 11.10 us in a stretch with a granted clock of 0.58, and matmuls at the lower clock are themselves part of that busy time. The rule behind rival F (the Trainium skill, same page, "A second HAM failure mode: psum-queue depth-cycling") isn't borne out by the stretch A7.7 to V3.7 of the changed kernel, whose groups cycle banks without identity matmuls at a granted clock of 1.00. But the runs don't refute it: about the same stretch (E.7 to V) had 0.72 in e7_late and 0.91 in banks_old, where one or two neighbours stand otherwise, and no run tells what decides.
- *The closing part.* Forecast V + 42, measured V + 42.9, and 5.4 us of gain against 4.2. From ps.0 to the end of product 0 it was 39.8 forecast and 41.4 measured. But the terms were not these. The four waits went, as foreseen (14.0 us). The new waits were put at 2 us, at hd.2 and hd.3; they are 2.20 at sd.2, 1.21 at lg.3, 1.02 at hd.1 and 0.97 at hd.3, 5.4 in all.
- *"The rows are there at V + 32.5, 9 us ahead of need"* is the step that failed. SyncE's issue came 1.6 us behind the forecast (V + 31.1, not 29.5). But the 2.8 us of landing in [rows 5] are those of the first load alone, once for each half of the tokens. The second load, with the rows of all tiles from the fifth on, has a row of its own. The DMA issues of before, 270 to 290 us (the size in the last row isn't the load's whole size):

```profile
stack<-x_scr SPq DMA_DIRECT2D x1, 256.0 KB, 3.0
...
stack<-x_scr SPq DMA_DIRECT2D x1, 0.5 KB, 7.3
```

  In the changed kernel they take 2.9 and 7.8. And the need was counted from the third tile, while the first group of four is turned at 265.1, and the second, ahead of tile 1 on PE, was awaited until 268.5, V + 39.6. The chain had about 1.2 us of slack, not 9, and rival C's condition was wrong with it: the scatters decide not once ps.0 ends later than V + 15, but once it starts a good microsecond behind the V + 1.5 that it has. It cost the forecast nothing, since VectorE's own chain was a little longer, which is luck, and it is the reason why T gained nothing from VectorE's earlier product in the second try.

## What to carry to other kernels

Where no engine is full, a first estimate is the work of the longest engine, stretch by stretch, times the slack factor of a stretch that already runs dense: here that put 63.6 us on what became 62.3, in one case and with some luck in which engine was named. An order for several in-order engines may not split by kind of work: here, either half of it put back gave back all of the middle's gain, while a cut in time (splice_e6, mid_old, tail_old) left the gain of the part that was kept. And find the one piece that releases the most (here the copy of the maxima ahead of the write to memory) and keep every wait out from ahead of it.

After the waits of one chain are taken out, ask for the next chain's slack against its first consumer, and for the landing of its last load, not its first.

## What the runs showed of the hardware

In stretches of identical order a lowered TensorE clock came with less than half of the time spent at it: 10.3 us more at 1.2 GHz with 2.5 us (mid_old, E.5 to E.7), 10.4 us more with 0.6 (before against before_no_identity, E.7 to V). Sixteen more identity matmuls of 0.22 us didn't hold the clock up in the execution that was profiled (0.84 and 0.64, where the profile of before shows 0.91 and 0.89), and 64 fewer changed the time of neither kernel by a measurable amount.

Of SyncE's two loads of routed rows, issued 0.7 us apart, the second landed almost 6 us behind the first: they took 2.9 and 8.1 us in two_moves. Why isn't shown. The second is the larger, with the rows of 19 tiles where the first has those of 4; and SyncE issues two weights of 2 MB right behind them. The transfer engines were 96% busy from 262 to 272 there, at 318 GB/s:

```profile
262.00:272.00 10.00, 4.57 (x22) 4.06 (x23) 7.60 (x25) 1.58 (x3) 6.56 (x13) 0.69 0.96 318
```

At the upper clock the same order took the same time to a few hundredths in every kernel: E.3 to E.6 was 36.29 to 36.32 us in all six kernels that had the new order and its identity matmuls there (204.64 - 168.33 in the changed one), so single traces do tell differences of a few tenths in such a stretch, where the whole program's runs differ by 1%.
